# Sorted expert rows carry token number and weight, and each expert tile is added into the output by an indirect store

## What is computed

```python
def _L1_ffn_ref(x, gate_w, w1, w2, w3, sw1, sw2, sw3):
    t = x.reshape(-1, DIM)
    scores = jax.nn.softmax(t @ gate_w.T, axis=-1)
    weights, indices = jax.lax.top_k(scores, TOP_K)        # 2 of 16 experts
    y = jnp.zeros_like(t)
    for e in range(N_EXPERTS):
        w_e = jnp.sum(jnp.where(indices == e, weights, 0.0), axis=-1)
        y = y + _swiglu(t, w1[e], w3[e], w2[e]) * w_e[:, None]
    z = _swiglu(t, sw1, sw3, sw2)                          # shared expert
    return (y + z).reshape(shape)
...
    x = x + jnp.tanh(g_ffn[1]) * _L1_ffn_ref(_layernorm(x, axis=-1), ...)
```

## Time and profile before

| | us |
|---|---|
| Median of 3 runs | 1042.82 (1039.86 to 1047.49) |
| The profiled execution, its time | 1041.82 |
| The profiled execution, its span | 1040.3 |
| Mean granted TensorE clock of the span | 0.965 |
| PE busy | 959.9 (92%) |
| DVE busy | 463.0 (45%) |
| ACT busy | 263.9 (25%) |
| POOL busy | 96.5 (9%) |

### The profile page before, as it was taken

How to read it: one execution, slowest core, us unless ns; L and a number is a source line. 1 busy time by engine, 2 the same in 40 slices (tenths; PEclk the granted TensorE clock), 3 DMA queues, 4 the chain that set the end, 5 groups by cost and what they waited for, 6 DMA issues and landing times.

```text
span 1040.3 us, 16990 instructions
## 1 busy us (share of the span) xinstructions
PE 959.9 (92%) x7151; PEld 733.4 (70%) x7152; DVE 463.0 (45%) x701; ACT 263.9 (25%) x401; POOL 96.5 (9%) x122
## 2 busy tenths in 40 slices
PE   4699999999999999779999999989999999999970
PEld 4678787878878787679996447977985455555540
DVE  5555455544544555973121447976414111112124
ACT  4433333233333324232111114332200011111100
POOL 0000000000000001100000003120001412211115
PEclk9899999999999999989999999999799999999995
DMA  8000010000100010430003008215103319876516
GB/s 314 1 31 32 1 32 1 32 32 1 72 2 31 2 60 24 173 151 1 1 1 122 1 0 298 107 55 196 55 1 114 141 45 325 293 274 241 175 40 212
DMA packets 25843, 95.92 MB, mean 92 GB/s; under 512 B 3251, under 2 KB 4275, under 8 KB 22707
## 3 DMA queue, kind: packets, MB, share of 16 engines
q1 hardware_dynamic: 18306, 69.02, 18.6%
q0 software_dynamic: 7472, 25.96, 7.1%
HBM read 76.35 MB, written 18.61 MB: 91 GB/s over the span
## 4 chain that ended last, share of the span: by engine, by line
PE 85%; DVE 8%; ACT 2%; issue 2%; DMA 1%; POOL 1%; POOLq 0%; SPq 0%; DVEq 0%; ACTq 0%
PE ps L513 17%; PE ps L514 16%; PE ps L515 16%; PE ps L898 10%; PE ps L767 6%; PE ps L908 5%; PE ps L593 4%; PE ps L874 4%; PE ps L576 3%; PE ps L787 1%; POOL arena L1740 1%; DVE stats L1229 1%; PE ps L889 1%; DVE arena L1239 1%; PE ps L915 1%
## 5 line engine op out<-in xcount | busy, mean ns | idle before, releaser
L513 PE MATMUL ps<-arena_r 128*125 128x512 f32 (+1 forms) x416 | 164.2, 395 | 10.1 <-DVE arena_r L1207 10.1
L514 PE MATMUL ps<-arena_r 128*125 128x512 f32 (+1 forms) x416 | 157.2, 378 | 0.0
L515 PE MATMUL ps<-arena_r 128*125 128x512 f32 (+1 forms) x416 | 156.9, 377 | 0.0
L513 PE MATMUL ps<-hT,arena_r 128*128 128x448 f32 (+1 forms) x368 | 139.5, 379 | 3.8 <-DVE hT L1246 3.8
L514 PE MATMUL ps<-hT,arena_r 128*128 128x448 f32 (+1 forms) x368 | 137.3, 373 | 0.0
L515 PE MATMUL ps<-hT,arena_r 128*128 128x448 f32 (+1 forms) x368 | 137.2, 373 | 0.0
L898 PE MATMUL ps<-arena 128*128 x336 | 103.1, 460 | 1.8 <-ACT arena L1176 1.0
L513 PEld LDWEIGHTS ps<-arena_r 128*125 128x125 f32 (+1 forms) x416 | 78.1, 188 | 27.2 <-DVE arena_r L1207 9.8
L962 ACT ACTIVATE arena<-arena,mbias,mscale 125x448 f32<-125x448 f32 x96 | 66.2, 752 | 99.3 <-DVE arena L1319 99.3
L515 PEld LDWEIGHTS ps<-arena_r 128*125 128x125 f32 (+1 forms) x416 | 78.0, 188 | 13.8
L514 PEld LDWEIGHTS ps<-arena_r 128*125 128x125 f32 (+1 forms) x416 | 78.2, 188 | 10.7
(11 more groups left out here) (186 smaller groups left out, 1198.4 us busy)
## 6 DMA issues: line engine op xcount, KB each, us to landing
arena<-in_e SPq DMA_DIRECT2D x16, 1408.0 KB, 6.5
arena<-in_e SPq DMA_DIRECT2D x16, 512.0 KB, 8.7
sorted_rows<-arena POOLq DMA_DIRECT2D x1, 7424.0 KB, 23.3
land_c<-in_ctx SPq DMA_DIRECT2D x8, 752.0 KB, 4.4
arena<-sorted_rows POOLq DMA_DIRECT2D x21, 256.0 KB, 6.4
sorted_rows<-arena POOLq DMA_DIRECT2D x21, 256.0 KB, 6.0
land_w<-in_gu SPq DMA_DIRECT2D x8, 512.0 KB, 4.5
arena<-in_e SPq DMA_DIRECT2D x16, 192.0 KB, 9.0
```

Source lines behind the costliest of these rows:

```text
L513: mm(into, a[0], w[0], start=i == 0, stop=False)
L514: mm(into, a[0], w[1], start=False, stop=False)
L515: last = mm(into, a[1], w[0], start=False, stop=i == len(operands) - 1)
```

## The change

A row of the sorted list is now 514 words: 512 values, the token's row in the output, and its weight. GpSimd writes the token number (plus 128) once by an iota, and the weight column before the scatter of each choice; the second choice's column is written after the first seven scatters have landed. The rows of the list that no token fills are zero; DVE takes the larger of the token number and the lane's number, so that such a row adds zeros to one of 128 spare rows that the output tensor has ahead of its 896.

GpSimd loads a tile directly into `xg`; the two staging buffers, the copies and the two buffers of products are gone. DVE copies token number and weight out of `xg` (`row_ends`), the weight is multiplied into the hidden rows, the product is evicted to a single buffer `yr`, and GpSimd adds it into the output in DRAM by an indirect DMA that accumulates (`scatter_add`). Each addition waits until the one before has landed. `x`, with the shared expert in it, is stored to the output by SP before the loop, as soon as each tile is complete. The gathers and sums at the end are gone.

```diff
+ROW = D + 2
...
-        A_E = A_KV
-        h3 = at(28160, NT, D)
-        xg = at(8904, D)
+        A_E = A_KV - 16
+        h3_row = at(28144, NT, ROW)
+        h3 = h3_row[:, :, 0:D]
+        xg = at(8888, ROW)
...
-        A_XR = A_SH
-        A_YR = A_SH + 2 * D
-        back = [[at(31744 + (2 * t + j) * D, D) for j in range(2)] for t in range(NT)]
+        yr = at(A_SH, D)
+        A_TOKEN = A_SH + D
+        weight = at(A_SH + D + 8, 1)
...
             post(0)
             post(1)
+            out_t = out[P:P + TOK, :].rearrange("(t p) d -> t p d", p=P)
+            for t in range(NT):
+                sp.wait_ge(y_sv, 3 * NT + t + 1)
+                sp.dma_start(out_t[t], x[:, t, :]).then_inc(x_st, 16)
...
-            out_t = out.rearrange("(t p) d -> t p d", p=P)
-            for t in range(NT):
-                sp.wait_ge(out_st, 1 + t)
-                sp.dma_start(out_t[t], x[:, t, :]).then_inc(x_ld, 16)
-            sp.wait_ge(x_ld, 16 * (NT + 1))
...
             def rows_T(n):
-                pe.wait_ge(xs_rdy, n + 1)
+                pe.wait_ge(xg_ld, n * 16 + 16)
...
-                v.tensor_tensor(hmoe[:, 0:EI], ps[:, 5, 0:EI], smoe, ALU.mult).then_inc(m_h, 1)
+                v.scalar_tensor_tensor(hmoe[:, 0:EI], ps[:, 5, 0:EI], weight, smoe, ALU.mult, ALU.mult).then_inc(m_h, 1)
+
+            def row_ends(n):
+                dve.wait_ge(xg_ld, n * 16 + 16)
+                if not (isinstance(n, int) and n == 0):
+                    dve.wait_ge(m_h, n)
+                v.tensor_tensor(arena[:, bass.ds(A_TOKEN + n % 4, 1)], xg[:, D:D + 1], lane[:], ALU.max)
+                v.tensor_copy(weight, xg[:, D + 1:D + 2]).then_inc(row_read, 1)
...
-                v.tensor_scalar(arena[:, bass.ds(A_YR + (n % 2) * D, D)], ps[:, 3, :], 1.0, None, ALU.mult
-                                ).then_inc(d_sv, 1)
-
+                v.tensor_copy(yr, ps[:, 3, :]).then_inc(d_sv, 1)
...
-            with dve.Fori(3, tiles) as n:
+            with dve.Fori(3, last1) as n:
                 tile_hidden(n)
-                tile_out(n - 1, n * 16 - 32)
+                row_ends(n + 1)
+                tile_out(n - 1, n * 16 - 16)
                 tile_hidden_save(n)
...
             for j in range(2):
+                if j == 1:
+                    pool.wait_ge(scattered, 16 * NT)
+                nc.gpsimd.tensor_copy(h3_row[:, :, D + 1], wtop[:, :, j]).then_inc(ids_set, 1)
+                pool.wait_ge(ids_set, 2 + j)
                 for t in range(NT):
                     pool.indirect_dma_start(xs_dram, bass.IndirectOffsetOnAxis(dest[:, j, t:t + 1], 0),
-                                            h3[:, t, :], None).then_inc(scattered, 16)
+                                            h3_row[:, t, :], None).then_inc(scattered, 16)
...
+            def load(n):
+                pool.dma_start(xg, xs_dram[bass.ds(n * P, P), :]).then_inc(xg_ld, 16)
+
+            def next_load(n):
+                pool.wait_ge(xg_tr, n)
+                pool.wait_ge(row_read, n)
+                load(n)
+
+            def scatter_add(n, stored=None):
                 pool.wait_ge(d_sv, n + 1)
                 if stored is not None:
                     pool.wait_ge(y_st, stored)
-                pool.dma_start(xs_dram[bass.ds(n * P, P), :], arena[:, bass.ds(A_YR + (n % 2) * D, D)]
-                               ).then_inc(y_st, 16)
+                nc.gpsimd.tensor_copy(token[:], arena[:, bass.ds(A_TOKEN + n % 4, 1)]).then_inc(token_set, 1)
+                pool.wait_ge(token_set, n + 1)
+                pool.sem_inc(token_held, 1)
+                pool.indirect_dma_start(out, bass.IndirectOffsetOnAxis(token[:, 0:1], 0), yr, None,
+                                        compute_op=ALU.add).then_inc(y_st, 16)
...
-            with pool.Fori(3, last1) as n:
-                pool.wait_ge(xg_ld, n * 16 + 16)
-                pool.wait_ge(xs_rdy, n)
-                load(n + 1)
-                pool.wait_ge(xg_tr, n)
-                place(n)
-                store(n - 2, n * 16 - 32)
...
+            next_load(1)
+            next_load(2)
+            pool.wait_ge(x_st, 16 * NT)
+            scatter_add(0)
+            next_load(3)
+            scatter_add(1, 16)
+            with pool.Fori(4, tiles) as n:
+                next_load(n)
+                scatter_add(n - 2, n * 16 - 32)
+            scatter_add(last2, last2 * 16)
+            scatter_add(last1, last1 * 16)
             pool.wait_ge(y_st, tiles * 16)
-            pool.sem_inc(pool_held, 1)
-
-            for t in range(NT):
-                for j in range(2):
-                    pool.indirect_dma_start(back[t][j], None, xs_dram,
-                                            bass.IndirectOffsetOnAxis(dest[:, j, t:t + 1], 0)).then_inc(back_ld[t], 16)
```

More of the change, by code:

```diff
@@ L99, in flamingo @@
         idx8 = sb("idx8", [P, NT, 8], U32)
+        token = sb("token", [P, 1], U32)
+        lane = sb("lane", [P, 1])
         WORDS = 48400
@@ L205, in flamingo @@
         qrelu = at(A_WH + 4096 + HALF, HALF)
[L206 to L207 removed]
+        zrec = [at(A_WH + 4096 + 2 * HALF, G, S), at(A_WH + 4096 + 3 * HALF + ROW, G, S)]
+        zero = at(A_WH + 4096 + 3 * HALF, ROW)
         gT = at(28160, KC, TOK)
@@ L255, in flamingo @@
         texpf = scratch(1704, 32)
-        xs_dram = nc.dram_tensor("sorted_rows", (ROWS_MAX * P, D), F32, kind="Internal").ap()
+        xs_dram = nc.dram_tensor("sorted_rows", (ROWS_MAX * P, ROW), F32, kind="Internal").ap()
         bv_ld = sem("bv_ld")
@@ L377, in flamingo @@
         e_ld = [sem(f"e_ld{i}") for i in range(NSLOT)]
-        back_ld = [sem(f"back_ld{t}") for t in range(NT)]
         block = stack.enter_context(nc.Block())
@@ L1618, in _ @@
             tile_hidden(2)
-            tile_out(1)
+            row_ends(3)
+            tile_out(1, 16)
             tile_hidden_save(2)
-            with dve.Fori(3, tiles) as n:
+            with dve.Fori(3, last1) as n:
                 tile_hidden(n)
-                tile_out(n - 1, n * 16 - 32)
+                row_ends(n + 1)
+                tile_out(n - 1, n * 16 - 16)
                 tile_hidden_save(n)
-            tile_out(last1, last2 * 16)
-            for t in range(NT):
-                dve.wait_ge(back_ld[t], 32)
-                for j in range(2):
-                    last = v.scalar_tensor_tensor(x[:, t, :], back[t][j], wtop[:, t, j:j + 1], x[:, t, :],
-                                                  ALU.mult, ALU.add)
-                    if j == 0:
-                        then(last)
-                last.then_inc(out_st, 1)
+            tile_hidden(last1)
+            tile_out(last2, last2 * 16)
+            tile_hidden_save(last1)
+            tile_out(last1, last1 * 16)
         @block.gpsimd
@@ L1640, in _ @@
             pool.wait_ge(pool_step, 1)
+            nc.gpsimd.iota(lane[:], pattern=[[0, 1]], base=0, channel_multiplier=1,
+                           allow_small_or_imprecise_dtypes=True)
             nc.gpsimd.affine_select(out=ident[:], in_=ident[:], compare_op=ALU.not_equal, fill=1.0, base=0,
@@ L1668, in _ @@
             pool.wait_ge(at_low, 8)
+            nc.gpsimd.iota(h3_row[:, :, D], pattern=[[P, NT]], base=P, channel_multiplier=1,
+                           allow_small_or_imprecise_dtypes=True).then_inc(ids_set, 1)
             nc.gpsimd.iota(iota16, pattern=[[1, NE]], base=0, channel_multiplier=0,
@@ L1692, in load @@
             def load(n):
-                pool.dma_start(arena[:, bass.ds(A_XR + (n % 2) * D, D)], xs_dram[bass.ds(n * P, P), :]
-                               ).then_inc(xg_ld, 16)
-            def place(n):
-                nc.gpsimd.tensor_copy(xg, arena[:, bass.ds(A_XR + (n % 2) * D, D)]).then_inc(xs_rdy, 1)
-            def store(n, stored=None):
+                pool.dma_start(xg, xs_dram[bass.ds(n * P, P), :]).then_inc(xg_ld, 16)
[4 more added lines that the diff above has]
+            def scatter_add(n, stored=None):
                 pool.wait_ge(d_sv, n + 1)
```

43 lines of the change are left out of this document (12 added, 31 removed).

## The result

| | before | after |
|---|---|---|
| median, us | 1043.73 (1039.86 to 1047.49, 4 runs) | 1154.04 (1150.1 to 1156.03, 4 runs) |
| profiled execution: span, time | 1040.3, 1041.8 | 1154.4, 1156.0 |
| tile 0's down to tile 18's down (18 intervals) | 148.5 | 280.9 |
| last tile's down to the end | 31.9 | 14.9 |
| granted clock, mean | 0.965 | 0.935 |

The ratio is 1.107, with an interval of 1.103 to 1.110: the change costs 110 us. The forecast was 1114, with a range of 1068 to 1145. Its sign and its mechanism were right, its size was too small by 40 us, and the result lies 9 us above the range.

The account below looks back on a forecast made before the run. TensorE, 85% of the chain that ended last, was taken as the bound. From 1041.8 us: tail -23.4, loop intervals +76.8, head +1, TensorE's clock +18, giving 1114 us, range 1068 to 1145.

Parts of the forecast that it names:

- Rival B: The change only removes the work after the loop, with loads landing 4.7 us after down or earlier; 1018 us, chance 0.05.
- the ring: Loop: load waits behind an older tile's addition and eviction, nothing overlapping from down to down; 76.8 us over 18 intervals.
- the price of the addition: Loop: bytes of the indirect addition, ahead of the load on the same queue, cost 0.1 to 0.2 us per interval.
- The quiet landing: Loop intervals without a weights fetch: load lands in 2.9 us plus the addition's bytes; interval 10.45, 2.2 over 8.25, six times.
- The clock: TensorE's clock halves in most long gaps beside weights: 1.5 us each, bounds 0 and 3.1, 18 in all; short gaps nothing.
- The landing beside weights: Twelve intervals with a weights fetch: load lands 10.0 us after down ends, bounds 9.8 and 10.6; 5.3 us over each.
- The start of the load, T + 3.9: Loop: T is the end of a tile's down; after eviction, token copy and indirect DMA the load starts 3.9 us later.
- PE's part, 3.5: Loop, after the load lands: transposes 0.45, exposed table read about 0.4, down 2.7; 3.5 us per interval.
- The tail, 8.5: After the last down: eviction, GpSimd's wake, token copy and additions landing in 4.3 us take 8.5 instead of 31.9; gain 23.4.
- The head, +1: Before the loop: second seven scatters wait for the first, load(0) starts at 827.7 instead of 823.47; 1 us added.
- rival A: Additions to DRAM are slow, holding the load 2 us longer in all 18 intervals, 36 us more: 1150; chance 0.12.
- Rival C: Beside weights the load gets a fair turn, landing 4.0 us after its start, cycle 11.4 in 12 intervals: 1076; chance 0.11.

Follow-up runs that it names:

- Experiment 1: Against after, only GpSimd's order changed: a tile's load is issued ahead of the addition it followed; 1031.68 us, 0.988 of before.
- experiment 6: After with the staging buffers back: 1046.37 us. Its last kernel also has the addition one turn later, token copy before the eviction wait, last wait on DVE: 1022.87.
- experiment 3: After with plain indirect stores in place of the adding ones, same rows and place; 1120.85 us, 1.074 of before.
- experiment 4: After with unread extra TensorE products before the row transposes: twelve 1220.61 us, five 1129.52; three, with small transfers for the fetches of experts 4 to 15, 1098.02.
- experiment 2: After with the weights fetches of experts 4 to 15 replaced by three transfers of 8 KB each; 1123.09 us, 1.076 of before.
- experiment 5: After with the last addition's landing awaited by DVE (and a one-column copy) instead of GpSimd; 1153.51 us, 1.106 of before.

## Why the prediction was right, and where it fell short

**The mechanism held.** The steps "down(n-2), eviction(n-2), scatter-add(n-2), load(n+1), transposes(n+1), down(n-1)" are the chain of after, row by row; PE waits 18 times, ahead of the row transposes, for that DMA; six intervals are short and twelve long. Experiment 1 undoes this order alone and takes back 122 us. Rival B (the tail alone, 1018) needed the ring open. The last kernel of experiment 6, where it is open and PE never waits in the loop, gives 1022.9; it also has the staging buffers back, so it is another program and only near to B's case.

**The size fell short by 41.7 us** (+114.1 in the span against +72.4). The step that failed is the price of the addition, "I add 0.1 to 0.2 for the addition's bytes". With plain stores in its place (experiment 3) the kernel takes 1120.9, 7 us over the forecast of 1114; the addition is worth the other 33. It acts twice: it delays the load behind it, and in the quiet intervals the longer gap also brings a lower clock (0.62 while down runs, in the interval from 1100.08), which the sum had at nothing. By terms, as they stand in the sum:

- *The quiet landing.* An addition was priced as bytes. The load behind it lands in 4.8 to 5.2 where the term had 3.05. Experiment 3 shows 3.2 behind a plain store. Per quiet interval +1.9; the early start below takes 0.7 back.
- *The clock, "For the six short gaps nothing".* They cost 1.5 each (experiment 4), and the twelve others 2.4 instead of 1.5: 9 + 11 = 20 us, half of the shortfall. The bounds of 0 and 3.1 held for the long gaps; that a gap of nearly 5 us would bring the clock down rested on the earlier trace rows alone, and the 1.5 taken between the bounds was an estimate that no run shows. After has gaps of 5.1 to 5.9 in the intervals beside a fetch and a granted clock of 0.79 to 0.80 in eleven of them, 0.89 in one. For gaps as short as the forecast had them, nothing was right: experiment 3 has 1.3 to 1.5 us there and the full clock in five of six. The quiet gaps of after are 2.8 to 3.3. I had no bound for the case that they come out longer, though the earlier trace rows had a stretch of 2.4 us, partly idle, with a granted clock of 0.51 behind it.
- *The landing beside weights, "nearer the first".* I took T + 10.0 between 9.8 and 10.6; after has 3.2 + 7.3 = T + 10.5. The end further away was the right one. With PE's longer part this is 0.7 in each of twelve, 8.5 us (14.26 at the full clock in experiment 4, where 8.25 + 5.3 had 13.55).
- *The start of the load, T + 3.9.* It is T + 3.2: GpSimd issues the load (929.07) while the indirect DMA of 928.01 is still counted as busy (1.62 us). Adding the two durations was wrong, by 0.7 in the good direction.
- *PE's part, 3.5.* At the full clock it is 0.66 + 0.40 + 2.85 = 3.9 (experiment 4). The earlier trace rows has 0.45 and 2.6 to 2.8 for products in a running stream; after a stall the same ones take more.
- *The tail, 8.5.* It is 14.9. Both additions take 4.9 to 5.0 instead of 4.3, and GpSimd's closing DRAIN stands 4.7 behind the last landing. Before has one too, but it started at 1019.7, 20 us ahead of the end, and was over with it at 1039.2, so the end didn't wait for it. The gain is 17.0 instead of 23.4.
- *The head, +1.* It is -1.1, where load(0) starts at 826.09 instead of 827.7; the heads of the traces differ by more than that.

Together: twelve intervals +19.1 over their term, six +18.4, tail +6.4, head -2.1, the two downs behind the loop -0.2; sum 41.6. Most of these errors go one way, and for one reason: each unknown was given the nearest row of a quiet, running pipeline (a gather, a stream of products, a transfer without an addition), and what was to be priced was the same thing in a stalled one. The range left out rival A as a separate case when it was a term that adds to the forecast; with A's 36 us the same sum gives 1150, and after took 1154. Two slips in the working changed little: the low end of the forecast, 1085, comes to 1093 from its own terms, and the quiet gap of 2.3 counts 0.4 of table read, which the 4.9 beside weights doesn't.

**Rival C** (a fair turn among the weights) was refuted in part. The load takes 7.3 beside a fetch and 4.9 alone: 2.4 more, less than the 3.4 to 4.3 of the earlier trace rows and more than C's 1.1. Behind a plain store it is 3.2 and 6.6 (experiment 3), 3.4 more. C's landing of 4.0 was an estimate that no run shows, and how the load shares the DMA engines with the fetch isn't shown either.

## What to carry to other kernels

Before a transfer is moved behind another one on the same engine's program, write down what the other waits for, and follow it until it closes on itself; here that order was worth 122 us, and with it undone the same transfers cost almost nothing. Where an operation has no row in the trace, as the addition here, don't price it by its bytes: it was worth 33 us inside the ring. If an indirect addition replaces a gather at the end, let it lag by one turn more than its eviction needs (15.5 us here), and keep the loads in their own buffers ahead of it. And when a chain stalls each turn, price its links from rows taken behind a stall, the clock's among them, not from a running stream.

## What the runs showed of the hardware

- An indirect addition of 128 rows of 2 KB landed in 4.7 to 5.0 us with the DMA engines otherwise quiet, the plain indirect store in 2.8; it occupied GpSimd 1.62 against 1.02, and a load behind it on the queue took 1.7 more to land (0.6 more beside a weights fetch).
- In the six quiet intervals of after TensorE waited 2.8 to 3.3 us for its rows, and the granted clock was 0.87 to 0.88 over the interval. In the twelve beside a fetch it waited 5.1 to 5.9, and the clock was 0.79 to 0.80 in eleven and 0.89 in one. Without fetches (experiment 2) the waits were 2.9 to 3.4 and the clock 0.87 to 0.88 in 17 intervals, but 1.00 in the first, with a wait of 2.88. With the plain store the quiet waits were 1.3 to 1.5 us, and the clock 1.00 in five of six intervals and 0.86 in one. With work of no use in the gap it was 1.00 over the loop (experiment 4), and five such products (4.3 us) made the kernel 24.5 us faster.
- GpSimd's closing DRAIN lasted 4.7 us behind the last landing where GpSimd had itself waited for it. Started ahead of the landing, it ended 2.4 us past it (experiment 5 and the last kernel of experiment 6).
- GpSimd issued a plain load 1.06 us after the start of an indirect DMA that the profile counts as 1.62 us long.
- A 128x512 product in float32 took 0.86 us at a granted clock of 1.00 (10.30 for twelve in experiment 4) and is two instructions in the profile.
